# Attention scores as three fp32r products over four heads, a new order of each batch's work, and weights split in place

## Time and profile before

| | us |
|---|---|
| runs, median (three) | 788.14 (785.09, 788.14, 793.72) |
| the profiled execution | 793.47 |
| its span, first to last instruction | 791.7 |
| PE, PEld busy | 682.0 (86%), 546.3 (69%) |
| DVE, ACT, POOL busy | 397.7 (50%), 278.5 (35%), 278.6 (35%) |
| TensorE's granted clock, mean | 0.961 of full speed |

### The profile page before, as it was taken

One profiled execution on the slowest core, in us unless ns is written; L12 is line 12 of the kernel. 1 busy time (PEld: TensorE's weight loads), 2 busy tenths in 40 slices (PEclk: granted clock), 3 DMA queues, 4 the chain that ended last, 5 costly groups with the idle time before them and its releaser, 6 DMA issues.

```text
span 791.7 us, 13422 instructions
## 1 busy us (share of the span) xinstructions
PE 682.0 (86%) x4865; PEld 546.3 (69%) x4866; DVE 397.7 (50%) x885; ACT 278.5 (35%) x494; POOL 278.6 (35%) x324
## 2 busy tenths in 40 slices
PE   0211999998989899998979999999799999999991
PEld 0201878786868687787858989999667766666760
DVE  7885334545555454445364599422434444444441
ACT  7453163635353442426373322444311111111110
POOL 1564022313222221223132111584634444555531
PEclk9999999999979889799999999999899999999997
DMA  8431000101010000102011543442555555555543
GB/s 293 133 114 45 1 2 1 54 2 53 0 53 0 26 26 0 53 0 81 1 64 43 218 131 115 133 147 85 209 129 102 104 106 103 101 99 98 104 66 40
DMA packets 24785, 62.07 MB, mean 78 GB/s; under 512 B 3056, under 2 KB 7152, under 8 KB 23728
## 3 DMA queue, kind: packets, MB, share of 16 engines
q1 hardware_dynamic: 15344, 41.16, 15.0%
q0 software_dynamic: 8736, 20.45, 14.3%
q10 hardware_dynamic: 672, 0.03, 0.1%
HBM read 38.56 MB, written 23.07 MB: 78 GB/s over the span
## 4 chain that ended last, share of the span: by engine, by line
PE 41%; DMA 24%; issue 15%; DVE 5%; POOL 4%; ACT 3%; POOLq 0%; DVEq 0%; ACTq 0%
DMA out_tokens<-yo,dest 23%; PE PS L1388 13%; PE scores L1388 11%; PE PS L1498 5%; PE scores L1630 5%; PE scores L1484 3%; POOL probs L514 2%; PE PS L1453 2%; POOL att_l L520 1%; DMA probs<-in_ws 1%; ACT probs L687 1%; ACT probs L691 1%; PE PS L1521 1%; DVE rden L1074 1%; POOL rstd L505 1%
## 5 line engine op out<-in xcount | busy, mean ns | idle before, releaser
L1388 PE MATMUL scores<-xb,sw 128*128 128x256 f32 x768 | 97.6, 283 | 0.0
L1388 PEld LDWEIGHTS scores<-xb,sw 128*128 128x128 f32 x768 | 95.1, 191 | 2.1 <-issue 0.4
L589 POOL DMA_INDIRECT out_tokens<-yo,dest x39 | 61.7, 1583 | 93.6 <-DMA out_tokens<-yo,dest 91.5
L514 POOL TENSOR_SCALAR_AFFINE_SELECT probs<-probs 128x256 f32<-128x256 f32 x128 | 51.2, 426 | 113.9 <-ACT probs L691 113.1
L1388 PE MATMUL PS<-xt_h,w_h 128*128 128x256 f32 x256 | 77.7, 303 | 1.5 <-DVE xt_l L1059 1.5
L687 ACT ACTIVATE probs<-scores 128x768 f32<-128x768 f32 x64 | 51.4, 803 | 75.9 <-PE scores L1484 75.9
L1711 PE MATMUL scores<-wd_sb,ehT 128*128 x156 | 73.5, 593 | 1.0 <-DVE ehT L1348 1.0
L1388 PE MATMUL PS<-xt_l,w_h 128*128 128x256 f32 x256 | 74.2, 290 | 0.0
L1388 PE MATMUL PS<-xt_h,w_l 128*128 128x256 f32 x256 | 73.9, 289 | 0.0
L1074 DVE RECIPROCAL rden<-PS 128x256 f32<-128x256 f32 x32 | 56.2, 1757 | 34.3 <-PE PS L1498 34.3
L805 ACT ACTIVATE es<-scores 128x256 f32<-128x256 f32 x39 | 14.9, 383 | 164.2 <-PE scores L1388 164.2
(11 more groups left out here) (270 smaller groups left out, 1386.8 us busy)
## 6 DMA issues: line engine op xcount, KB each, us to landing
wgu_l<-in_wgu SPq DMA_DIRECT2D x8, 1024.0 KB, 6.7
T<-in_x SPq DMA_DIRECT2D x8, 512.0 KB, 8.0
probs<-in_wqkvo SPq DMA_DIRECT2D x8, 512.0 KB, 3.6
x_rows<-x SPq DMA_DIRECT2D x8, 512.0 KB, 2.9
x_cols<-x2T SPq DMA_DIRECT2D x8, 512.0 KB, 2.6
xc<-x_cols SPq DMA_DIRECT2D x8, 512.0 KB, 3.6
out_tokens<-T SPq DMA_DIRECT2D x8, 512.0 KB, 7.4
wd_sb<-in_wd SPq DMA_DIRECT2D x8, 512.0 KB, 6.7
```

Source lines behind the costliest of these rows:

```text
L514: ins = pool.affine_select(out=t, in_=t, compare_op=ALU.is_ge, fill=0.0, base=0, pattern=[[0, 2], [1, P]], channel_multiplier=-1)
L589: pool.indirect_dma_start(out[:, :], bass.IndirectOffsetOnAxis(dest[:, t:t + 1], 0), yo[:, t % 3, :], None, compute_op=ALU.add).then_inc(y ...
L1388: ins = pe.matmul(out, lhs(k, a), rhs(k, b), start=m == 0, stop=m == len(products) - 1)
```

## The change

1. **Scores.** `qT` and `kT` become `q_h`, `q_l`, `k_h`, `k_l` (fp32r). `head_scores` makes four heads at once, each in a strip of 32 rows and a bank of its own, from three fp32r products: 24 matmuls for each of four groups c. ACT rounds each projection (`qk_high`, new), DVE's copy becomes the subtraction. tanh, exp and mask handle four heads in one instruction (128x1536 values; `probs` holds two groups instead of four pairs).
2. **Order of a batch.** The scores of groups 0, 1, 2 of batch b+1 and its `head_values` 0 and 1 move into step b, between the values projections and the two halves of the output projection. Step b begins with group 3 of its own batch. The transposes of b+2 (`front_transposes`), ACT's `xt_high` and DVE's `xt_low` move to the end of step b. The sums of the second layer norm are taken apart (`second_sums`, `token_variances`, `second_normed`), with `xt_low` and a `normalise` between them.
3. **Weights in place.** The 8 attention chunks are loaded straight into the place of their low parts (no stage, no wait on SP). The shared expert's gate and up matrices are loaded at once (2 MB) and split in 8 pieces of 128x512 during attention (ACT `shared_high`, DVE `shared_low`). Its down matrix is loaded in the last step, behind the last tanh, and split there (ACT two halves, POOL `down_matrix_low` ahead of `hidden_low`); TensorE waits for it ahead of `down_chunk(0, 0)`.
4. **Start.** `ACT_STATS` 3 to 4; `BY_DVE` 896 to 640 columns, `BY_ACT` 640 to 896. An exponential of two values is put on ACT's queue behind the last round, ahead of the wait for `z_ready`.

```diff
-ACT_STATS = 3
+ACT_STATS = 4
-BY_DVE, BY_ACT = 7 * P, 5 * P
+BY_DVE, BY_ACT = 5 * P, 7 * P
+PIECE = 256
...
-STEP = ["XN0", "XN1", "X2T0", "X2T1", "GT", "Q0", "K0", "Q1", "K1", "V0", "V1", "YT0", "YT1", "OP0", "OP1"]
+STEP = ["Q0", "X2T0", "X2T1", "K0", "GT", "Q1", "K1", "YT0", "YT1", "V0", "V1", "OP0", "OP1", "XN0", "XN1"]
...
@@ SP
             for k in range(NW):
-                if k >= 3:
-                    sp.wait_ge(wlo_done, k - 2)
-                sp.dma_start(stage[:, k % 3, :], chunk_of(k, wqkvo, ws)).then_inc(stage_loaded[k % 3], 16)
+                sp.dma_start(chunk_of(k, w_raw), chunk_of(k, wqkvo)).then_inc(w_loaded[k], 16)
+            for j in range(2):
+                sp.dma_start(sw_raw[:, j, :], ws[:, j, :]).then_inc(shared_loaded, 16)
...
             load_tokens(1)
+            sp.wait_ge(tanh_done, 4 * B)
+            sp.dma_start(sw_raw[:, 2, :], ws[:, 2, :]).then_inc(down_loaded, 16)
             store_x2(B - 1)
@@ POOL
+            def step(b, has_front, has_next):
+                mask(b, 3)
                 att_low(b, 1)
                 att_low(b, 2)
                 att_low(b, 3)
                 if has_next:
                     rstd_of(var1_ready, rstd1_ready, b + 2)
+                if has_front:
+                    mask(b + 1, 0)
+                    mask(b + 1, 1)
+                    mask(b + 1, 2)
+                    att_low(b + 1, 0)
+                else:
+                    down_matrix_low()
                     hidden_low(0, 0)
                     hidden_low(0, 1)
                 rstd_of(var2_ready, rstd2_ready, b)
@@ ACT
-            for m in range(8 + ROUNDS, 2 * NW):
-                weight_high_half(m)
+            act.activation(qf[:, 480:482], powers[:, 0:2], ACT.Exp).then_inc(act_step, 1)
             act.wait_ge(z_ready, 1)
...
+            def qk_high(part, item, s):
+                act.wait_ge(*filled(part, item, s))
+                k, _ = ring(part, item, s)
+                act.activation(heads_of(q_h if item[0] == "Q" else k_h, item), ring_bank[k],
+                               ACT.Copy).then_inc(qk_h_done, 1)
...
+                soft(b, 3)
+                if has_front:
+                    qk_high(part, "Q0", b)
+                else:
                     split_high(0, 0)
+                att_high(b, 1)
                 if has_back:
                     x2_transposed(part, b)
                 att_high(b, 2)
+                if has_front:
+                    qk_high(part, "K0", b)
+                    shared_high(b)
+                    qk_high(part, "Q1", b)
+                    qk_high(part, "K1", b)
                 att_high(b, 3)
+                if not has_front:
+                    down_matrix_high()
                 if has_next:
                     tokens(part, b + 2, b)
+                if has_front:
+                    soft(b + 1, 0)
+                    values(part, b, 0)
+                    soft(b + 1, 1)
+                    values(part, b, 1)
+                    soft(b + 1, 2)
+                    act.wait_ge(*filled(part, "OP1", b))
+                    att_high(b + 1, 0)
+                if has_next:
+                    xt_high(part, b)
@@ DVE, end of a step
+                add_projection(part, b, 0)
+                if has_front:
+                    normalise(b + 1, 0)
+                add_projection(part, b, 1)
+                second_sums(part, b)
+                if has_next:
+                    xt_low(part, b + 2, b)
+                token_variances(var2_ready)
+                if has_front:
+                    normalise(b + 1, 1)
+                second_normed(b, first)
@@ TensorE
+            def head_scores(b, c, first=False):
+                if not (first and c == 0):
+                    pe.wait_ge(tanh_done, 4 * b + c)
                 for tt in range(TT):
-                    for h in (2 * p, 2 * p + 1):
-                        bank, c, r = score_bank[2 * (p % 2) + h % 2], h // HC, D * (h % HC)
-                        ins = pe.matmul(bank[:, tt * S:S + tt * P], kT[r:r + D, c, tt * P:(tt + 1) * P],
-                                        qT[r:r + D, c, tt * P:S], start=True, stop=True)
+                    for m, (k_of, q_of) in enumerate(((k_h, q_h), (k_h, q_l), (k_l, q_h))):
+                        for j in range(HC):
+                            r = D * j
+                            ins = pe.matmul(score_bank[j][:, tt * S:S + tt * P], k_of[r:r + D, c, tt * P:(tt + 1) * P],
+                                            q_of[r:r + D, c, tt * P:S], start=m == 0, stop=m == 2)
                 ins.then_inc(scores_full, 1)
...
+                head_scores(b, 3)
                 if has_front:
+                    if isinstance(b, int) and b == 0:
+                        front_split("ahead", 0)
+                    else:
+                        front_split("mid", b - 1)
+                    heads_projection(part, "Q0", b)
+                head_values(b, 2)
                 if has_back:
                     gate_transposes(part, b - 1, b)
+                if has_front:
+                    heads_projection(part, "K0", b)
+                else:
+                    pe.wait_ge(tanh_done, 4 * b + 4)
+                    pe.wait_ge(xb_l_done, 1)
+                    pe.wait_ge(piece_low, 8)
+                    hidden_chunk(0, 0, True, 0)
                 if has_back:
                     gate_partial(part, b)
                 if has_front:
+                    heads_projection(part, "Q1", b)
+                if has_back:
+                    gate_logits(part, b - 1, b)
+                head_values(b, 3)
                 if has_front:
                     heads_projection(part, "K1", b)
+                else:
+                    hidden_chunk(0, 1, True, 0)
                 if has_next:
                     y_transposes(part, b + 2, b)
+                if has_front:
+                    pe.wait_ge(*emptied(part, "K0", b))
+                    head_scores(b + 1, 0)
+                    values_projection(part, b, 0)
+                    head_scores(b + 1, 1)
+                    values_projection(part, b, 1)
+                out_projection(part, b, 0)
+                if has_front:
+                    pe.wait_ge(*emptied(part, "K1", b))
+                    head_scores(b + 1, 2)
+                    pe.wait_ge(*emptied(part, "V1", b))
+                    head_values(b + 1, 0)
+                out_projection(part, b, 1)
+                if has_next:
+                    front_transposes(part, b + 2, b)
+                if has_front:
+                    head_values(b + 1, 1)
...
-            pe.wait_ge(tanh_done, 8 * B)
+            pe.wait_ge(tanh_done, 4 * B)
+            pe.wait_ge(down_low, 2)
             down_chunk(0, 0, True)
```

More of the change, by code:

```diff
@@ L614, in _ @@
             na = CB * ACT_STATS
-            unread = [t[:, S * k:S * (k + 1)] for t in (front, x2T, x2) for k in range(CB)]
+            unread = [t[:, S * k:S * (k + 1)] for t in (front, x2T, x2, vf) for k in range(CB)]
             for b, k, c in cols:
@@ L674, in xt_high, with values @@
                                    ACT.Copy).then_inc(xt_h_done, 1)
[L676 to L688, removed]
-                               scale=1.0 / (np.sqrt(D) * SOFTCAP)).then_inc(tanh_done, 1)
-                act.wait_ge(tanh_done, 8 * b + p + 1)
-                act.activation(probs[:, p % 4, :], probs[:, p % 4, :], ACT.Exp, scale=SOFTCAP).then_inc(exp_done, 1)
+            def values(part, s, tt):
+                act.wait_ge(*filled(part, f"V{tt}", s))
+                k, _ = ring(part, f"V{tt}", s)
+                act.activation(v[:, tt, :], ring_bank[k], ACT.Copy).then_inc(ring_free[k], 1)
@@ new lines, in soft @@
+            def soft(b, c, first=False):
+                act.wait_ge(scores_full, 4 * b + c + 1)
+                if not (first and c < 2):
+                    act.wait_ge(pv_done, 4 * b + c - 1)
+                act.activation(of_four(c), scores[:, 0:HC, 0:384], ACT.Tanh,
+                               scale=1.0 / (np.sqrt(D) * SOFTCAP)).then_inc(tanh_done, 1)
+                act.wait_ge(tanh_done, 4 * b + c + 1)
+                act.activation(of_four(c), of_four(c), ACT.Exp, scale=SOFTCAP).then_inc(exp_done, 1)
@@ new lines, in qk_high, with shared_high @@
+            def qk_high(part, item, s):
[3 more added lines that the diff above has]
+                               ACT.Copy).then_inc(qk_h_done, 1)
+            def shared_high(b):
+                for m in pieces(b):
+                    if isinstance(b, int):
+                        act.wait_ge(shared_loaded, 32)
+                    act.activation(piece_of(m, sw_h), piece_of(m, sw_raw), ACT.Copy).then_inc(piece_high, 1)
@@ L693, in att_high, with down_matrix_high @@
+            def down_matrix_high():
+                act.wait_ge(down_loaded, 16)
+                for h in range(2):
+                    act.activation(sw_h[:, 2, 1024 * h:1024 * (h + 1)],
```

(29 more changed lines are left out.)

251 lines of the change are left out of this document (125 added, 126 removed).

## The result

The changed kernel takes 744.35 us (median of four runs, 742.5 to 745.9), the kernel before 786.63 beside it (785.09 to 793.72): a ratio of 0.9445 with a 95% interval of 0.9381 to 0.9508, 42.3 us less. The prediction was 746. The profiled execution took 744.2, its span 742.5.

What follows compares the result with a forecast made beforehand. The prediction took TensorE's queue, with its idle time and half clock behind waits, to bound attention, small DVE and ACT chains the start. Gains 12.0 + 7.1 + 5.8 + 16.8 = 41.7 gave 746 us against the median; range 731 to 769.

Steps and rivals of the forecast that it cites:

- Start: Stage before attention, to 80.67: median, small DVE instructions and table load together gain 12.0 us.
- The median: Start: moving count columns from DVE to ACT gains 0.3 us for each of 8 rounds, 2.5 us.
- The five small instructions: Start, DVE behind the median: moving POOL's subtractions away gains 7.8 us; rival that they stay slow: 754, chance 0.06.
- The table: Start, ACT: loading the exponential's table beforehand gains 1.7 us.
- Scores: Attention, TensorE: 32 groups of 24 matmuls at 1.07 us, 34.2 instead of 41.3, gain 7.1 us.
- Idle time: Attention: TensorE's idle time falls from 18.9 to 13.1 us, gain 5.8.
- The point against the change: Attention: eight new two-input DVE pieces and POOL's masks exclude each other, at most one mask for each piece.
- Clock: Attention: 20.8 us lost to half clock behind TensorE's waits; 4 left, gain 16.8 us.
- Strips in turn: Rival, scores: fp32r row strips run one after the other, 3.07 us a group, 64 more, 810; chance 0.07.
- strips at the full rate: Rival, scores: four row strips in little more than one matmul's time, 0.6 us a group, 731; chance 0.07.
- The clock doesn't stay low: Answers the rival that attention's clock falls despite short waits, so 16.8 and the idle gain are lost: 769; chance 0.18.
- DVE at a step's end: Attention: 0.4 us a step allowed; rival that DVE's chain becomes the bound, 2 us in 7 steps: 760, chance 0.12.

Runs made afterwards that it cites:

- the filled and unfilled waits: Changed kernel with next batch's scores 0 to 2 and first two values together behind the projections: 808.46 us; same with unused matmuls in its three waits per step: 794.72.
- the fp32 scores: Changed kernel with q and k kept in plain fp32, four heads at once, 8 matmuls a group instead of 24 fp32r ones: 743.78 us.
- the filled kernel: Changed kernel with next batch's scores 0 to 2 and first two values together behind the projections, unused matmuls put into three waits per step: 794.72 us.

## Why the prediction was right

The mechanism was right in every stage but for the cause of one small gain; one term was mis-sized, and that the number agrees better than its sum is luck.

- **Start**, 12.0 predicted, 13.1 measured. The median, 2.5 predicted (0.3 for 8 rounds is 2.4): 2.1 by the old shares put back. The fourth image, counted at nothing: the first count on ACT begins 0.9 earlier, at 29.98 instead of 30.91; that the image does it no run shows. The five small instructions, 7.8 predicted: about 8.6 with a sixth (L983, from 0.69 to 0.16), with POOL as the cause, as the equal ends in the earlier trace rows said. The table, 1.7: 1.6 by the two timelines, but the added exponential has no part in it (above).
- **Scores**, 7.1 predicted, 32 x (1.29 - 0.84) = 14.4 measured, with 41.3 / 32 = 1.29 before. This is the term that failed. "I take 1.07, one pass per matmul as there" went by records, from the values in column strips. The nearer row stood in the same group: 16 fp32 records over four *row* strips in 0.88, the very shapes of a group. The prediction used that row by its records too, as 1.32. A group is six passes of four strips, 0.84 / 6 = 0.14 each on average.
- **Idle time**, 5.8 predicted, 18.85 - 13.55 = 5.3 measured. The last step has 25.92 - 19.39 = 6.5 (6.4 predicted), a middle step 0.55 (0.4) where it was looked for: `xt_low` behind the sums. The point against the change didn't come up: the eight DVE pieces took 0.68 us each, and no POOL mask ran beside one.
- **Clock**, 16.8 predicted. TensorE's busy time fell by 29.8, less 14.4 for the scores: 15.4. It was forecast as a thing of waits, and the filled and unfilled waits bear that out.
- **The sum** was 41.7; between the two profiled executions it is 49.3, and 7.3 of the 7.6 missing are the scores. That 746 is still near 744.35 comes from a second thing: the profiled execution of before lies 793.47 - 786.63 = 6.8 above its median, that of after on its own. Set against the median, the sum of the profile was bound to come out too large, and the undersized scores hid it: two errors that cancel. The clocks on record point to the clock term: executions of before with a mean granted clock of 0.961, as the profiled one has, took 793.1 to 793.2 us, one with 0.971 took 787.0, those with 0.976 took 784.7 to 785.4, one with 0.982 took 780.5. If so, 42.3 - 13.1 - 14.4 - 5.3 - 1.0 = 8.5 us are left for the clock against the median, an estimate. This stays open: those with 0.945 or 0.946 took no longer (783.4 to 785.3), and no trace of any of these was kept. In the fp32 scores a start at 0.75 brings the mean to 0.962 and costs no time, so the mean alone doesn't tell.
- **Rivals.** Strips in turn (3.07 a group) and strips at the full rate (0.6) are both excluded by 0.84. The clock doesn't stay low: it is 0.99 in attention. DVE at a step's end costs 0.55, not 2. The small instructions are slow only with POOL beside them.

## What to carry to other kernels

When a matmul fills only a strip, count passes over the columns with all strips side by side, and take the price from the row with the same strips, not from the number of records. Put dense work of the next batch between the links of a chain that crosses engines: the wait itself is only part of what it costs, as several in a row brought the clock down here too. And look for long POOL instructions beside any chain of tiny DVE ones.

## What was not expected of the hardware

- POOL fills without an SBUF input held DVE's TENSOR_SCALAR rows (0.18 to 1.84, four of `front` from 1.38 to 6.08) and left TENSOR_TENSOR rows of the same sizes alone (0.15, 0.26).
- In fp32r, four strips with three products cost 0.84 a group, in fp32 0.87: in strips the extra precision of plain fp32 costs nothing here.
- Waits of 1.93 us in equal places brought the clock down in some steps and not in others; one of 1.63 in each step of the filled kernel never did. What decides this stays open.
